# A graph-attention kernel with x, the adjacency and the weights also laid out by columns, and 13 of 16 batches normalized by features

## The reference

```python
def _layernorm(x, axis=-1, eps=1e-05):
    m = jnp.mean(x, axis=axis, keepdims=True)
    v = jnp.var(x, axis=axis, keepdims=True)
    return (x - m) / jnp.sqrt(v + eps)

def _gat(inp, adj_mask, W, a):          # alpha = 0.2
    h = jnp.matmul(inp, W)
    f1 = jnp.matmul(h, a[:F_, 0])
    f2 = jnp.matmul(h, a[F_:, 0])
    e = jax.nn.leaky_relu(f1[:, :, None] + f2[:, None, :], ALPHA)
    if adj_mask is not None:
        e = jnp.where(adj_mask[None, :, :] > 0, e, NEG_INF)
    att = jax.nn.softmax(e, axis=2)
    return jax.nn.elu(jnp.einsum('bij,bjf->bif', att, h))

def _L0_gnn_ref(x, adj, ...):
    out = jax.nn.relu(jnp.matmul(x, mlp1_w) + mlp1_b)      # 128 -> 256
    residual = out
    out = _gat(jax.nn.relu(out), None, W_fc, a_fc)         # attention 1, no mask
    out = jax.nn.elu(out) + residual
    out = jax.nn.relu(jnp.matmul(out, mlp2_w) + mlp2_b)    # 256 -> 128
    residual = out
    out = _gat(jax.nn.relu(out), adj, W_hand, a_hand)      # attention 2
    return jax.nn.relu(jax.nn.elu(out) + residual)

h = jnp.maximum(_layernorm(x, axis=-1), 0.0)
x = x + _L0_gnn_ref(h, adj, ...)
h = jnp.maximum(_layernorm(x, axis=-1), 0.0)
x = x + _L1_gnn_ref(h, adj, L1_gnn_W, L1_gnn_a)            # attention 3, masked
```

## Time and profile before

| | |
|---|---|
| median of 3 runs | 454.4 us (452.09 to 455.82) |
| the profiled execution: time, span | 451.98 us, 450.2 us |
| PE busy | 425.7 us, 95% |
| DVE busy | 356.5 us, 79% |
| ACT busy | 326.0 us, 72% |
| POOL busy | 25.0 us, 6% |
| mean granted clock of PE | 0.986 |
| moved by DMA | 24.42 MB, 54 GB/s on average |

### The profile page before, as it was taken

How to read it: one execution, slowest core, us unless ns; L and a number is a source line. 1 busy time by engine, 2 the same in 40 slices (tenths; PEclk the granted TensorE clock), 3 DMA queues, 4 the chain that set the end, 5 groups by cost and what they waited for, 6 DMA issues and landing times.

```text
span 450.2 us, 8759 instructions
## 1 busy us (share of the span) xinstructions
PE 425.7 (95%) x2601; PEld 363.4 (81%) x2601; DVE 356.5 (79%) x1246; ACT 326.0 (72%) x780; POOL 25.0 (6%) x53
## 2 busy tenths in 40 slices
PE   5999999999999999999999999999999999996853
PEld 4678779887787889888898879988888989885843
DVE  7785577876788869699998787997778897899854
ACT  3556748868696967688877788668865868888842
POOL 0100000000100100000100010000000000000000
PEclk9999999999999999999999999999999999997989
DMA  7310100101121242210233022031022110410001
GB/s 219 96 48 1 49 23 25 41 9 23 42 78 39 60 117 71 64 33 15 81 95 93 26 62 82 25 94 42 11 71 92 23 48 3 118 49 24 25 1 52
DMA packets 33257, 24.42 MB, mean 54 GB/s; under 512 B 2603, under 2 KB 28086, under 8 KB 33206
## 3 DMA queue, kind: packets, MB, share of 16 engines
q1 hardware_dynamic: 31824, 22.23, 17.3%
q10 hardware_dynamic: 1382, 1.58, 1.2%
HBM read 19.54 MB, written 4.27 MB: 53 GB/s over the span
## 4 chain that ended last, share of the span: by engine, by line
PE 60%; DVE 4%; ACT 2%; issue 2%; DVEq 0%; ACTq 0%
PE bank L1390 20%; PE bank L1304 15%; PE bank L1293 8%; PE bank L1340 5%; PE bank L1322 3%; PE bank L1284 3%; PE bank L1312 2%; PE bank L1358 1%; PE bank L1398 1%; DVE stats L930 1%; ACT prob L760 1%; PE bank L1276 1%; DVE u L971 1%; DVE u L1123 1%; ACT y L801 1%
## 5 line engine op out<-in xcount | busy, mean ns | idle before, releaser
L1390 PEld LDWEIGHTS bank<-ext,prob 128*128 128x128 f32 x1024 | 122.3, 194 | 9.5 <-issue 6.4
L1390 PE MATMUL bank<-ext,prob 128*128 128x129 f32 x1024 | 125.9, 278 | 2.8 <-DVE prob L1064 2.1
L1304 PE MATMUL bank<-ext,prob 128*128 128x257 f32 x512 | 119.0, 380 | 0.0
L1304 PEld LDWEIGHTS bank<-ext,prob 128*128 128x128 f32 x512 | 94.2, 190 | 15.2 <-issue 2.8
L1071 DVE SCALAR_TENSOR_TENSOR prob<-prob,square,mask_t 128x512 f32<-128x512 f32 x96 | 69.0, 741 | 3.7 <-ACT prob L760 3.6
L760 ACT ACTIVATE prob<-row,square 128x512 f32<-128x512 f32 x96 | 66.1, 717 | 2.4 <-DMA row<-row_scratch 2.3
L1293 PE MATMUL bank<-wfc_sb,o_t 128*128 128x259 f32 x256 | 63.8, 383 | 0.8 <-ACT o_t L698 0.7
L1123 DVE SCALAR_TENSOR_TENSOR u<-e,y 128x512 f32<-128x512 f32 (+1 forms) x70 | 44.5, 639 | 17.7 <-ACT e L813 14.0
L1293 PEld LDWEIGHTS bank<-wfc_sb,o_t 128*128 128x128 f32 x256 | 46.4, 190 | 11.0 <-issue 4.8
L801 ACT ACTIVATE y<-bank,recip 128x128 f32<-128x128 f32 x128 | 39.0, 364 | 17.5 <-DVE recip L1115 14.9
L809 ACT ACTIVATE e<-y,minus_one 128x512 f32<-128x512 f32 (+1 forms) x70 | 47.8, 684 | 1.3
...
...
## 6 DMA issues: line engine op xcount, KB each, us to landing
row<-row_scratch SPq DMA_DIRECT2D x36, 256.0 KB, 3.4
x_in<-in_x SPq DMA_DIRECT2D x16, 256.0 KB, 3.0
x_res<-in_x SPq DMA_DIRECT2D x16, 256.0 KB, 3.9
out<-y_out SPq DMA_DIRECT2D x16, 256.0 KB, 3.7
...
adj_sb<-in_adj ACTq DMA_DIRECT2D x1, 1024.0 KB, 6.1
wfc_sb<-in_L_gnn_W_fc ACTq DMA_DIRECT2D x1, 256.0 KB, 4.1
...
```

The costliest lines, as they stand in the source:

```text
L1304: last = nc.tensor.matmul(filled[:, 0:H + 1], gat1.targets(b, t, c), gat1.features_and_one(b, t), start=(t == 0), stop=(t == C - 1))
L1390: last = nc.tensor.matmul(filled[:, e * (D + 3):e * (D + 3) + D + 1], L.targets(b, t, c), L.features_and_one(b, t), start=(t == 0), stop=( ...
```

## The change

The host hands over second copies: x with features ahead of nodes (x_t), the adjacency and three weights transposed, and all vectors as columns of one array. The transposes of weights and vectors on PE, with their ACT copies, are gone, and so are the mask's: a two-input DVE operation now compares the transposed adjacency with 0 and takes the maximum with a row of "empty" that PE spreads by four transposes into PSUM ("empties").

Batches 0, 1 and 2 (TURNED) are normalized as before. For the 13 others "norm1" ends with a DVE block transpose of means and roots; "row0" on SP writes them to a scratch and reads them back, broadcast to all partitions (4 KB each); "load_t" loads x by columns; "normt" on DVE subtracts the row of means and applies relu and the row of roots, straight into normed_t. "turn1" is left out for these batches on PE and ACT. The ORDER table is new for all engines.

```diff
+TURNED = (0, 1, 2)
 ORDER = {
     "sync": """
-        load.0 load.1 weights load.2 load.3 load.4 load_again.0 load.5 load.6 load_again.1 load.7 load.8 load.9
+        load.0 load.1 weights load_again.0 load.2 load_again.1 load.3 load_t.3 load.4 load_t.4 load.5 row0.3
...
+            def load_x_by_features(b):
+                if b.n - 2 in TURNED:
+                    sp.wait_ge(*norm_filled[0].at(Batch.nth(b.n - 2), 1))
+                elif b.n - 2 in BY_FEATURES:
+                    sp.wait_ge(*norm_t_made.two_back(b))
+                sp.dma_start(x_by_features[:, b.slot], x_t[b.n]).then_inc(x_t_loaded.sem(b), 16)
+
+            def spread_moments(b):
+                sp.wait_ge(*moments_turned.at(b, 1))
+                if b.n - 2 in BY_FEATURES:
+                    sp.wait_ge(*moments_loaded.two_back(b))
+                rows = moments_scratch[b.slot].rearrange("(m k i) -> k m i", m=2 * C, k=ROWS)
+                for k in range(ROWS):
+                    sp.dma_start(rows[k], moments_t[32 * k:32 * k + 2 * C, b.slot]).then_inc(
+                        moments_written.sem(b), 16)
+                sp.wait_ge(*moments_written.landed(b))
+                if b.n - 2 in BY_FEATURES:
+                    sp.wait_ge(*norm_t_made.two_back(b))
+                sp.dma_start(moments_row[:, b.slot].rearrange("p c m i -> p (c m i)"),
+                             moments_scratch[b.slot].rearrange("(o n) -> o n", o=1).broadcast_to([P, 2 * N])).then_inc(
+                    moments_loaded.sem(b), 16)
...
+                act.dma_start(vec_sb[:], vectors).then_inc(s_vec, 16)
+                act.dma_start(turned_w[:, 0:4].rearrange("p (k j) n -> p k j n", k=HT),
+                              wfc_t.rearrange("(j p) (k n) -> p k j n", p=P, k=HT)).then_inc(s_turned1, 16)
                 act.dma_start(wfc_sb[:, :, 3:H + 3], wfc.rearrange("(k p) f -> p k f", p=P)).then_inc(s_wfc, 16)
...
+                act.dma_start(turned_w[:, 4], whand_t).then_inc(s_turned23, 16)
+                act.dma_start(turned_w[:, 5], wl1_t).then_inc(s_turned23, 16)
+                act.dma_start(adj_sb[:], adj.rearrange("(c p) j -> p c j", c=C)).then_inc(s_adj, 16)
+                act.dma_start(adj_t_sb, adj_t.rearrange("(c p) j -> p c j", c=C)).then_inc(s_adj_t, 16)
+                act.dma_start(w2_sb[:], w2.rearrange("(k p) f -> p k f", p=P)).then_inc(s_w2, 16)
...
-            def edges(b):
                 dve.wait_ge(s_adj, 16)
-                nc.vector.tensor_scalar(edge, adj_sb[:], 0.0, None, ALU.is_gt).then_inc(s_mask, 1)
...
-            def mask(b, c):
-                dve.wait_ge(s_mask, 3)
-                nc.vector.tensor_scalar(edge_or_empty[:, c, :], edge[:, c, :], empty[:, c:c + 1], None,
-                                        ALU.max).then_inc(s_mask, 1)
+            def mask(b, t):
+                if t == 0:
+                    dve.wait_ge(s_adj_t, 16)
+                    dve.wait_ge(s_empty, 1)
+                nc.vector.scalar_tensor_tensor(out=mask_t[:, t], in0=adj_t_sb[:, t], scalar=0.0,
+                                               in1=bank_of("empties", b)[:], op0=ALU.is_gt, op1=ALU.max).then_inc(
+                    s_mc, 1)
...
                 newton_step(b, 0)
                 dve.wait_ge(*rstd_ready[0].at(b, 1))
-                if b.first > 0:
+                if not turned(b):
+                    if b.n - 2 in BY_FEATURES:
+                        dve.wait_ge(*moments_loaded.two_back(b))
+                    nc.vector.transpose(moments_t[:, b.slot], moments_n[:, b.slot]).then_inc(moments_turned.sem, 1)
+                    return
...
+            def norm_by_features(b):
+                row, centre = moments_row[:, b.slot], x_by_features[:, b.slot].rearrange("p (c i) -> p c i", c=C)
+                dve.wait_ge(*moments_loaded.landed(b))
+                dve.wait_ge(*x_t_loaded.landed(b))
+                nc.vector.tensor_tensor(centre, centre, row[:, :, 0], ALU.subtract).then_inc(centred.sem, 1)
+                dve.wait_ge(*centred.at(b, 1))
+                dve.wait_ge(*o1_filled.two_back(b))
+                nc.vector.scalar_tensor_tensor(out=normed_t[0][:, b.slot].rearrange("p (c i) -> p c i", c=C),
+                                               in0=centre, scalar=0.0, in1=row[:, :, 1], op0=ALU.max,
+                                               op1=ALU.mult).then_inc(norm_t_made.sem, 1)
...
             def mlp1(b, f):
                 if b.first == 0 and f == 0:
                     pe.wait_ge(s_w1, 16)
-                pe.wait_ge(*norm_t_ready[0].at(b, 1))
+                pe.wait_ge(*x_normed(b))
```

More of the change, by code:

```diff
@@ new lines @@
+        args3.0 att1_1.4 row1.5 norm2.1 att1_2.4 z_1.3 max2.2 prob3_0.0 args2.2 prob1_0.5 prob1_1.5 norm1.11
+        att1_3.4 prob1_2.5 prob1_3.5 stats1.13 elu1_0.4 row2.2 att1_0.5 max2.3 root2n.1 prob3_1.0 args2.3
+        prob3_2.0 row2.3 prob3_3.0 elu1_1.4 att1_1.5 att1_2.5 max3.1 z_0.4 att1_3.5 z_1.4 args3.1 prob2_0.2
+        prob2_1.2 elu1_0.5 att3_0.0 prob2_2.2 row3.1 elu1_1.5 att3_1.0 prob2_3.2 normt.8 prob2_0.3 prob2_1.3
+        att2_0.2 z_0.5 z_1.5 elu3.0 prob2_2.3 att2_1.2 prob3_0.1 prob2_3.3 result.0 elu2.2 max2.4 x1.2 args2.4
@@ new lines @@
+        norm2.2 att2_0.3 row2.4 prob3_1.1 prob3_2.1 prob3_3.1 att2_1.3 max2.5 norm1.12 root2n.2 args2.5 row2.5
+        max1.6 att3_0.1 args1.6 normt.9 prob2_0.4 att3_1.1 row1.6 prob2_1.4 prob2_2.4 max3.2 stats1.14 args3.2
+        prob2_3.4 row3.2 normt.10 elu3.1 prob2_0.5 prob1_0.6 prob1_1.6 prob1_2.6 prob1_3.6 prob2_1.5 prob2_2.5
+        att2_0.4 att1_0.6 max1.7 elu2.3 prob2_3.5 prob3_0.2 args1.7 prob3_1.2 att1_1.6 result.1 att1_2.6
+        att2_1.4 x1.3 prob3_2.2 prob3_3.2 norm2.3 root2n.3 att1_3.6 row1.7 norm1.13 elu2.4 elu1_0.6 elu1_1.6
@@ new lines @@
+        att2_0.5 stats1.15 att3_0.2 max3.3 att2_1.5 args3.3 att3_1.2 z_0.6 row3.3 prob1_0.7 prob1_1.7 elu3.2
+        z_1.6 max1.8 prob1_2.7 prob1_3.7 result.2 x1.4 args1.8 norm2.4 row1.8 root2n.4 att1_0.7 prob3_0.3
+        prob3_1.3 att1_1.7 prob3_2.3 prob3_3.3 normt.11 norm1.14 max3.4 att3_0.3 max2.6 prob1_0.8 att1_2.7
+        args2.6 att3_1.3 prob1_1.8 elu2.5 args3.4 att1_3.7 row2.6 prob1_2.8 prob1_3.8 elu3.3 result.3 elu1_0.7
+        x1.5 max1.9 row3.4 elu1_1.7 args1.9 norm2.5 root2n.5 z_0.7 att1_0.8 z_1.7 att1_1.8 prob2_0.6 row1.9
@@ new lines @@
+        prob2_1.6 prob2_2.6 prob3_0.4 prob2_3.6 att1_2.8 max3.5 att2_0.6 prob3_1.4 prob3_2.4 args3.5 row3.5
+        prob1_0.9 att2_1.6 prob3_3.4 normt.12 prob1_1.9 max2.7 att1_3.8 norm1.15 att3_0.4 args2.7 elu1_0.8
+        row2.7 elu2.6 prob1_2.9 prob3_0.5 att3_1.4 prob3_1.5 prob1_3.9 prob3_2.5 max1.10 prob3_3.5 elu1_1.8
+        elu3.4 result.4 att3_0.5 args1.10 row1.10 x1.6 att1_0.9 att1_1.9 norm2.6 prob2_0.7 att1_2.9 z_0.8
+        elu1_0.9 z_1.8 root2n.6 prob2_1.7 att1_3.9 prob1_0.10 prob2_2.7 prob2_3.7 att3_1.5 max3.6 prob1_1.10
```

501 lines of the change are left out of this document (235 added, 266 removed).

## The result

The changed kernel took 439.1 us (median of four, 438.8 to 440.7) beside 455.1 us of the kernel before on the same chip: a ratio of 0.967, 95% interval 0.961 to 0.972. On another chip it took 439.8 (438.8 to 441.0) beside 453.4, 0.971 (0.968 to 0.974). It is faster, as forecast, and by more: 445.1 was said, and 439.1 lies just outside the range's low end of 439.5. The profiled execution took 439.2 us, its span is 437.3 us, 12.9 shorter than that of before, where my sum said 9.3.

A forecast was written before the change was run, and what follows sets the result against it. PE was taken to bound 25 to 394 us. Terms 5.7 + 1.3 + 1.5 + 2.0 - 1.2 = 9.3 us off the profiled 452.0 gave 442.7, plus 2.4 to the median: 445.1 us, 8-in-10 range 439.5 to 451.5.

The forecast's parts named there:

- What bounds the kernel: From 25 to 394 us PE is the limit, busy 367.8 of 369.0 us, so PE work removed there shortens the program.
- The transposes and masks: PE loses the x transposes of 13 batches, 5.7 us, and 12 mask transposes net, 1.3 us, all counted as gain.
- The start: Before 25 us, weight transposes go and the first "h1" comes near 13 us: gain 1.5, ends 2.9 and -1.5.
- DVE's stalls: From 25 to 394 us, 6.5 us of added DVE work costs PE 1.2 us; bounds 0 and 6.5.
- the late load of batch 2: At the start, x of batch 2 lands late behind other loads; the start then gives nothing or costs 1.5 us.
- The new DMA chain: Per batch, column load, writes and broadcast take 5.6 to 8.3 us, hidden behind over 7 us of DVE work: 0.
- The tail: After 394 us, the new order takes some 5 us of DVE work out: gain 2.0, ends -2 and 5.
- no loss of clock in the tail: Rival: PE no longer waits before the last "row2", keeps its high clock, some 3.5 us more gain, 441.6; chance 0.12.
- The step from profile to median: Whole program: the median is 2.4 us above the profiled execution, so 442.7 becomes 445.1 us.
- DVE as the bound: Rival: in the middle nearly all of DVE's added 6.5 us shows, sum 4.0, time 450.4; chance 0.14.
- Free transposes: Rival: PE would have waited there anyway, 5.7 falls to 1 or 2, 449.5; chance 0.06, shared with a late start.
- SyncE's queue: Rival: "row0" steps hold the in-order queue 2.5 us each, delaying attention rows; six of 13 give 460.1; chance 0.06.

The follow-up runs named there:

- the run with the filling: The changed kernel with 26 unread transposes of the identity on TensorE between h3_1.14 and row3.14, where it waits for ScalarE: 438.8 us, ratio 0.967.

## Why the prediction came out as it did

**What bounds the kernel** was read rightly. The middle is PE's: it lost 0.2 us of 355, and 52 transposes put back cost 5.1 us for 5.7 worked out. Put back one at a time, the transposes (5.1) and the old tail (7.3) make up 12.4 of the 12.9 us between the profiles.

**The transposes and masks,** 5.7 + 1.3 = 7.0, hold in the main: the run with 52 transposes shows 5.1 of the 5.7, the 1.3 stand by count alone. "z_1.15" began 6.6 us sooner, with 0.9 us more of batch 13's work ahead of it in the new order: 7.5 in all. With 7.0 for this work, 0.5 is left for the next two terms.

**The start (1.5) and DVE's stalls (-1.2)** were both wrong, by 2.0 and 2.2 us, and by luck made up for each other. The first "h1" came at 13.7 as said (near 13) and batch 1's at 22.7, where I had said 19. By the PE work done up to the first attention I estimate the start at -0.5. What I had weighed as the late load of batch 2 happened (2.37 us of wait), and ScalarE's ten issues, which I hadn't priced at all, cost the rest. The run with the lighter start, which changed both and the warm-up, got 3.4 us back. The stalls came to -0.2 against 1.2 lost before, a gain of 1.0. The bounds named were 0 and 6.5, and I took the added load as a cost because DVE's share rose; but the new order is also one in which PE is fuller. That the added load does cost is shown apart: 2.4 us for 8.8.

**The new DMA chain** at 0: right, nobody waited for it in the changed kernel. The chain is no small thing, though. The two kernels in the old order show what it can cost where it stands wrongly: one "row0" ahead of one row put that off by 2.3 us, and with the slower transfers around it PE stood 4.1 us.

**The tail** was the mis-sized term: 2.0, with 5 as the better end. The stretch is 6.3 us shorter, 5.4 after the 0.9 us of work that now stands ahead of it; the old tail put back costs 7.3. I had found the 5 us of DVE work leaving the stretch and then took 3 off for "att3_0.14" at the low clock. The runs show that this subtraction was far too large: "att3_0.14" fills a place in which PE would wait, and even the full clock there, in the run with the filling, ends the kernel at most 1.1 us sooner. A reading beside it was off as well: I set 28 us of DVE work against "PE's 19 us there", where PE was busy 25.2 of the 32.8 us from 397.3 to 430.1. The rival "no loss of clock in the tail" didn't come about: the wait stayed (3.1 us) and the clock was lost. Of its 3.5 us the clock's part is at most 1.1; what the wait itself would have given, no run shows.

**The step from profile to median** failed too. I carried the 2.4 us between the profiled execution of before and its median over to the changed kernel. It belongs to the clock in the old tail, whose last 20 us differ by 2.7 us between two profiles. The changed kernel's first profiled execution lies at its median; its second, at 438.8, lies 1.0 below, so of the 2.4 us at most 1.0 carries over, and which execution is profiled is chance. The tail and this step are the two causes of the miss: 3.4 and 2.4 of the 6.0 us.

**The rivals.** DVE as the bound is out for this load, by the run with more of its work, though a quarter of that showed. Free transposes are out. SyncE's queue wasn't in the way here, and was in another order. DVE's busy time rose by 3.7 and not 6 to 7: the groups of the normalization give +5.9 (9.0 + 8.8, 13 block transposes of 0.21, less 13 x 1.12), and all other groups together -0.9. The groups overlap at their ends and so sum to more than the engine's busy time (403.4 against 360.2 us); the 1.3 us between +5.0 by groups and +3.7 by the engine lie there.

**Still open:** what the change is worth without any new order. My two attempts at it are slower than the kernel before for reasons of their own; that the order is needed is shown, its share isn't.
